# 128-wide attention: ScalarE in place of VectorE multiplies the exponentials by the reciprocal sums

## The chip, the cores and the metric

The kernel runs on one core of a Trainium2 chip. The metric is the device time of one execution in microseconds (us). Engines are written as the profile writes them: PE is TensorE, DVE is VectorE, ACT is ScalarE, POOL is GpSimd, SP is SyncE.

## What is computed

A decoder of two layers works on x, 16 sequences of 64 tokens of width 256, that is 1024 tokens or 8 tiles of 128 rows. It runs a self attention, a cross attention and a mixture of experts, then a causal attention, the attention that the change touches, and a second mixture of experts. The attention in question, cut to its core (H = 16 query heads, 4 key heads, HD = 128, 128 keys for each sequence: 64 of the context and 64 of its own):

```
q = rope(rms_norm(h @ Wq.T))           # 16 heads of 128
k = rope(rms_norm([ctx, h] @ Wk.T))    # 4 heads of 128
v = [ctx, h] @ Wv.T
scores = q @ k.T / sqrt(128)
probs  = softmax(scores)               # over the 128 keys
x      = x + (probs @ v) @ Wo.T
```

## The kernel before

`attention128` goes over the 8 tiles of 128 rows (two sequences each). Each engine has one program, written out by hand, and the engines meet at semaphores. `skewed` builds them: `early` for tile 0, then seven times `mixed(n, u, n1, u1)`, then `late` for tile 7. `mixed` handles the scores, softmax, values and projection of tile n interwoven with the projections, rope and transposes of tile n1 = n + 1. So in a period of `mixed` each engine works through a fixed list, in order, and an instruction that waits holds back everything behind it on its engine.

The softmax of a tile runs in four groups k = 0..3 of four head blocks of 128 x 128:

- PE `scores(n, k)` writes the bank `xps`; DVE `maxes(n, k)` (L1088, L1090) writes the negated scaled maxima `xnb`; ACT `exps(n, k)` (L798) computes four exponentials of 128 x 128 from PSUM into `E` (`xE` in the profile) with the bias per partition, and each leaves its row sum in `sm` by a second small instruction (ACTIVATION_READ_ACCUMULATOR), then raises `exp_ok`.
- DVE `normalise(n, k)` waits for `exp_ok`, takes the reciprocal of four sums (L1095, `rc_ok`), and multiplies the whole group, 128 x 512, by it in place (L1097), then raises `e_ok`.
- PE `turn_probs(n, k)` (L913) waits for `e_ok`, and for `t_out`, and transposes the four blocks into one of two PSUM banks `xpt`. ACT `pt_copy(n, k)` (L765, `xPT<-xpt`) copies them out and raises `t_out`. PE `pv(n, k)` (L925) multiplies by V; ACT `o_copy` (L808) copies that out; PE `project` (L933) applies Wo.

The two banks `xpt` are shared by all transposes of a period in a fixed order: the two key groups, the groups 0, 1 and 2 of the probabilities, a query group, group 3 of the probabilities, two more query groups, the next hidden tile, the last query group. Each transpose number j waits until copy number j - 2 is out, so `turn_probs(n, 3)` waits for `pt_copy(n, 2)`, and the query transpose behind it, `turn_qk(n1, 1)` (L943), for the query copy `qk_out` before it; that one also waits for `scale(n1, 1)` on DVE (L1083).

On ACT the second half of a period runs in this order: `exps(n, 2)`, `o_copy(n, 1)`, `square(n1, 6)` (L788), `exps(n, 3)`, `pt_copy(n, 2)`, `qk_out` 0, `v_copy(n1, 7)`, `pt_copy(n, 3)`. On PE: `turn_probs(n, 1)`, `pv` 0, `scores` 2, `pv` 1, `scores` 3, `fill(n1, 6)` (L896, six matmuls), `turn_probs(n, 2)`, `turn_qk(n1, 0)`, `fill(n1, 7)`, `turn_probs(n, 3)`, `turn_qk(n1, 1)`, `pv` 2.

POOL adds the two halves of the rope (`add`, L733, 128 x 512 from SBUF to SBUF) and takes the roots (L738, L727) in order.

Of the kernel before, what the change touches and what calls it, by code (L numbers as in the profile page):

```python
# [14 lines left out]
ALU = mybir.AluOpType  # L15
ACT = mybir.ActivationFunctionType
# [19 lines left out]
class Store:  # L36
# [7 lines left out]
    def sb(self, name, shape, dt=F32):  # L44
        return self.stack.enter_context(self.nc.sbuf_tensor(name, shape, dt))
# [18 lines left out]
def bcast(ap, axis, n):  # L64

    shape = list(ap.shape)
    shape.insert(axis, n)
    return ap.unsqueeze(axis).to_broadcast(shape)
# [475 lines left out]
KEYS = 2 * S  # L544
# [10 lines left out]
class Split:  # L555
# [9 lines left out]
    def share(self, n):  # L565
        return bass.ds(n * (self.COLS // NT), self.COLS // NT)
# [99 lines left out]
def attention128(nc, C, w):  # L666
# [5 lines left out]
    with m.stack:  # L672
# [16 lines left out]
        E = sb("xE", [P, XH, KEYS])  # L689
# [3 lines left out]
        rc = sb("xrc", [P, XH])  # L693
# [16 lines left out]
        def turns(n, u):  # L710

            base = n * STEP_T + FIRST_T
            if type(n) is int and n == NT - 1:
                base -= 1
                return base, lambda k: (base + k) % 2
            return base, lambda k: (u + k) % 2
# [6 lines left out]
        @block.gpsimd  # L723
        def _(pool):
            def root(n, u):
                pool.wait_ge(var_ok, n + 1)
                pool.tensor_tensor(mv[:, u, 3:4], mv[:, u, 2:3], neghalf[:, 0:1], ALU.pow).then_inc(rstd_ok, 1)  # L727

            def add(n, k):

                pool.wait_ge(rope_ok, n * 6 + k + 1)
                blk = qr[:, 4 * k:4 * k + 4, :]
                pool.tensor_tensor(blk, blk, t2[:, k % 2, :, :], ALU.add).then_inc(add_ok, 1)  # L733

            def rms_root(n, part):
                pool.wait_ge(ms_ok, n * 2 + part + 1)
                c = RMS[part]
                pool.tensor_tensor(sr[:, c], sv[:, c], neghalf[:, 0:1].to_broadcast([P, c.stop - c.start]), ALU.pow).then_inc(sr_ok, 1)  # L738

            def step(n1, u1):  # L740

                for k in range(4):
                    add(n1, k)
                rms_root(n1, 0)
                add(n1, 4)
                if type(n1) is not int or 1 <= n1 < NT - 1:
                    root(n1 + 1, 1 - u1)
                add(n1, 5)
                rms_root(n1, 1)

            root(0, 0)
            root(1, 1)
            step(0, 0)
            step(1, 1)
            with pool.Fori(0, (NT - 4) // 2) as i:
                step(i * 2 + 2, 0)
                step(i * 2 + 3, 1)
            step(NT - 2, 0)
            step(NT - 1, 1)

        @block.scalar
        def _(act):
            def turned(j, dst, src):
                act.wait_ge(t_ok, j + 1)
                act.activation(dst, src, ACT.Copy).then_inc(t_out, 1)  # L765

            def own(t):

                return t.rearrange("p c (b k) -> p c b k", b=2)

            def h_out(n, u, j, bank):

                act.wait_ge(t_ok, j + 1)
                act.activation(hs[:, u, 0, :, :], p_t[bank][:, 0:DC, :], ACT.Copy, scale=H_UP)
                act.activation(kv[:, u, 0, :, :, S:KEYS], own(p_t[bank][:, 0:DC, :]), ACT.Copy, scale=H_UP).then_inc(high_ok, 1)
                act.activation(kv[:, u, 0, :, :, 0:S], own(ctxT[:, :, bass.ds(n * P, P)]), ACT.Copy, scale=H_UP).then_inc(chigh_ok, 1)

            def qk_out(j, i, bank):
                if i < 4:
                    dst = QT[:, :, 4 * i:4 * i + 4, :]  # L780
                    turned(j, dst.rearrange("p b h q -> p h b q"), p_t[bank][:, :, :].rearrange("p h (b q) -> p h b q", b=2))
                else:
                    turned(j, KT[:, 4 * (i - 4):4 * (i - 4) + 4, :], p_t[bank][:, :, :])

            def square(n, k):

                act.wait_ge(r_ok, n * 8 + k + 1)
                act.activation(sq[:, SQI[k] % 2, :, :], p_r[k % 2][:, :, :], ACT.Square).then_inc(sq_ok, 1)  # L788

            def v_copy(n, u, k):  # L790
                act.wait_ge(r_ok, n * 8 + k + 1)
                act.activation(V[:, u, (k - 5) // 2, :, :], p_r[k % 2][:, :, :], ACT.Copy, scale=1.0 / (H_UP * W_UP)).then_inc(v_out, 1)

            def exps(n, k):
                act.wait_ge(nb_ok, n * 4 + k + 1)
                for i in range(4):
                    c = 4 * k + i
                    ins = act.activation(E[:, c, :], p_s[k % 2][:, i, :], ACT.Exp, bias=nb[:, c:c + 1], scale=XSCALE,  # L798
                                         accum_out=sm[:, c:c + 1])
                ins.then_inc(exp_ok, 1)  # L800

            def pt_copy(n, k, j, bank):
                turned(j, PT[:, k % 2, :, :], p_t[bank][:, :, :])

            def o_copy(n, u, k):

                act.wait_ge(o_ok, n * 4 + k + 1)
                act.activation(OT[:, 8 * (k % 2):8 * (k % 2) + 8, k // 2, :],  # L808
                               p_o[(u + k) % 2][:, :].rearrange("p (h q) -> p h q", q=S), ACT.Copy).then_inc(o_out, 1)

            def early(n, u):
                h_out(0, 0, 0, 0)
                for k in (0, 1, 2, 3, 4):
                    square(0, k)
                    if k == 1:
                        h_out(1, 1, 1, 1)
                v_copy(0, 0, 5)
                square(0, 6)
                v_copy(0, 0, 7)
                act.wait_ge(t_out, 2)  # L820
                for i in range(4):
                    qk_out(2 + i, i, i % 2)

            def mixed(n, u, n1, u1):
                base, bank = turns(n, u)
                square(n1, 0)
                qk_out(base + T_K[0], 4, bank(T_K[0]))
                square(n1, 1)
                qk_out(base + T_K[1], 5, bank(T_K[1]))
                square(n1, 2)  # L830
                exps(n, 0)
                square(n1, 3)
                exps(n, 1)
                square(n1, 4)
                pt_copy(n, 0, base + T_P[0], bank(T_P[0]))
                v_copy(n1, u1, 5)
                pt_copy(n, 1, base + T_P[1], bank(T_P[1]))
                o_copy(n, u, 0)
                exps(n, 2)
                o_copy(n, u, 1)  # L840
                square(n1, 6)
                exps(n, 3)
                pt_copy(n, 2, base + T_P[2], bank(T_P[2]))
                qk_out(base + T_Q[0], 0, bank(T_Q[0]))
                v_copy(n1, u1, 7)
                pt_copy(n, 3, base + T_P[3], bank(T_P[3]))
                qk_out(base + T_Q[1], 1, bank(T_Q[1]))
                o_copy(n, u, 2)
                qk_out(base + T_Q[2], 2, bank(T_Q[2]))
                if there(n + 2):  # L850
                    h_out(n + 2, u, base + T_H, bank(T_H))
                o_copy(n, u, 3)
                if there(n + 2):
                    act.wait_ge(t_out, base + T_H + 1)
                qk_out(base + t_q(n, 3), 3, bank(t_q(n, 3)))

            def late(n, u):
                base, bank = turns(n, u)
                qk_out(base, 4, bank(0))
                qk_out(base + 1, 5, bank(1))  # L860
                exps(n, 0)
                exps(n, 1)
                pt_copy(n, 0, base + 2, bank(2))
                pt_copy(n, 1, base + 3, bank(3))
                o_copy(n, u, 0)
                exps(n, 2)
                o_copy(n, u, 1)
                exps(n, 3)
                pt_copy(n, 2, base + 4, bank(4))
                pt_copy(n, 3, base + 5, bank(5))  # L870
                o_copy(n, u, 2)
                o_copy(n, u, 3)

            skewed(act, early, mixed, late)
# [154 lines left out]
        def _(dve):  # L1029
# [62 lines left out]
            def normalise(n, k):  # L1092
                c = slice(4 * k, 4 * k + 4)
                dve.wait_ge(exp_ok, n * 4 + k + 1)
                dve.reciprocal(rc[:, c], sm[:, c]).then_inc(rc_ok, 1)  # L1095
                dve.wait_ge(rc_ok, n * 4 + k + 1)
                dve.tensor_tensor(E[:, c, :], E[:, c, :], bcast(rc[:, c], 2, KEYS), ALU.mult).then_inc(e_ok, 1)  # L1097

            def residual(n, u):
                dve.wait_ge(proj_ok, n + 1)  # L1100
# [1168 lines left out]
```

## Time and profile before

| | us |
|---|---|
| median of 3 runs | 1067.71 (1065.79 to 1068.55) |
| the profiled execution | 1067.61 |
| its span, first to last instruction | 1065.8 |
| PE busy | 827.1 |
| DVE busy | 720.8 |
| ACT busy | 486.7 |
| POOL busy | 383.0 |

All durations below are from the one profiled execution; 1.8 us of its time lie outside its span. The attention that is touched runs from about 472 us to 763 us of the span. A row of the timeline gives start and length; a row with x4 is four instructions in a row, and the pitch of an engine is the distance from one start to the next, which is shorter than a length because consecutive instructions overlap.

### The profile page before, as it was taken

The page shows a single profiled execution, that of the slowest core. Times are in us where ns is not written, and L with a number is a line of the kernel's source. Part 1 is how long each engine was busy: PE and PEld are TensorE (multiplying, and loading weights), DVE is VectorE, ACT ScalarE, POOL GpSimd, SP SyncE. Part 2 cuts the span into 40 slices and gives each one's busy share as a digit, 9 for nine tenths or more (in the row PEclk, how much of TensorE's full clock was granted, in tenths as well). Part 3 has the DMA queues.
Part 4 walks back from the last instruction along what each step waited for, and adds up shares of the span by engine and source line. Part 5 has one row for each costly group of instructions (what it writes and reads, how often), then busy time and mean ns, then how long its engine had stood idle before and what let it go on. Part 6 is the DMA issues. An engine that isn't in the chain of part 4 may idle for free. (4 is left out here: it accounts for less than half of the span.)

```text
span 1065.8 us, 17161 instructions
## 1 busy us (share of the span) xinstructions
PE 827.1 (78%) x5527; PEld 542.3 (51%) x5534; DVE 720.8 (68%) x1503; ACT 486.7 (46%) x1241; POOL 383.0 (36%) x345
## 2 busy tenths in 40 slices
PE   3899752347777248957799888997549999999997
PEld 2777642216666136733567666676434444444443
DVE  3778956557999359837887788874355656656555
ACT  1765432114555225623654556555244554445453
POOL 1113763673555455505444344531021122121210
PEclk9999975568999669968999999999759999999999
DMA  9900001226988212000000000000106344343431
GB/s 312 419 15 2 2 2 60 80 76 207 283 264 273 84 45 58 22 1 1 1 1 1 1 0 0 1 1 1 48 11 172 109 123 119 109 133 103 133 94 40
DMA packets 49344, 90.63 MB, mean 85 GB/s; under 512 B 7046, under 2 KB 30089, under 8 KB 48778
## 3 DMA queue, kind: packets, MB, share of 16 engines
q1 hardware_dynamic: 46218, 81.63, 24.6%
q0 software_dynamic: 3072, 8.30, 2.5%
q8 instruction: 31, 0.51, 0.2%
q14 instruction: 23, 0.19, 0.1%
HBM read 67.71 MB, written 22.29 MB: 84 GB/s over the span
## 5 line engine op out<-in xcount | busy, mean ns | idle before, releaser
L1199 POOL TENSOR_TENSOR m1ws<-m1raw,m1ws 128x768 f16<-128x768 f32 x33 | 55.0, 1669 | 219.2 <-ACT m1raw L1202 219.2
L733 POOL TENSOR_TENSOR xqr<-xqr,xt 128x512 f32<-128x512 f32 x48 | 61.3, 1277 | 140.1 <-DVE xt L1069 140.1
L1509 DVE TENSOR_TENSOR m1sg<-m1sg,m1Wb 128x512 f32<-128x512 f32 x66 | 61.5, 931 | 63.5 <-ACT m1sg L1427 52.8
L1469 PE MATMUL m1pg<-m1hs,m1ws 128*128 128x512 f16 x396 | 97.5, 383 | 3.8 <-PEq L58 3.8
L1480 PE MATMUL m1py<-m1ap,m1ws 128*128 128x512 f16 x396 | 96.3, 379 | 1.4 <-DVE m1ap L1521 1.4
L1469 PE MATMUL m1pu<-m1hs,m1ws 128*128 128x512 f16 x396 | 97.1, 382 | 0.0
L1431 ACT ACTIVATE m1ap<-m1ac 128x512 f16<-128x512 f32 x66 | 41.6, 630 | 116.8 <-DVE m1ac L1515 116.8
L1521 DVE TENSOR_TENSOR m1ap<-m1ac,m1ap 128x512 f16<-128x512 f32 x66 | 45.7, 692 | 45.9 <-ACT m1ap L1431 45.9
L1469 PEld LDWEIGHTS m1pg<-m1hs,m1ws 128*128 128x128 f16 x396 | 38.9, 98 | 51.3 <-issue 5.3
L1480 PEld LDWEIGHTS m1py<-m1ap,m1ws 128*128 128x128 f16 x396 | 38.6, 98 | 48.7 <-DVE m1ap L1521 2.4
L1469 PEld LDWEIGHTS m1pu<-m1hs,m1ws 128*128 128x128 f16 x396 | 39.0, 99 | 47.7 <-issue 1.6
L788 ACT ACTIVATE xsq<-xpr 128x512 f32<-128x512 f32 x48 | 28.8, 601 | 75.3 <-PE xpr L896 75.3
L933 PE MATMUL xpo<-xwo,xOT 128*128 128x256 f32 x256 | 59.6, 380 | 0.7 <-ACT xOT L808 0.7
L1065 DVE TENSOR_REDUCE xss<-xsq 128x4 f32<-128x512 f32 x48 | 32.7, 682 | 35.1 <-ACT xsq L788 34.6
L798 ACT ACTIVATE xE<-xps,xnb 128x128 f32<-128x128 f32 x128 | 45.5, 380 | 23.5 <-DVE xnb L1090 23.5
L896 PE MATMUL xpr<-xparts,xhs 128*128 128x512 f16 x192 | 49.4, 397 | 8.1 <-DVE xkv L1049 5.2
L933 PEld LDWEIGHTS xpo<-xwo,xOT 128*128 128x128 f32 x256 | 47.1, 190 | 7.5 <-ACT xOT L808 1.3
L896 PE MATMUL xpr<-xparts,xkv 128*128 128x512 f16 x192 | 47.6, 387 | 3.4 <-DVE xt L1069 3.4
L2026 PE MATMUL m0ph<-m0xs,m0wg 128*128 128x256 f16 x384 | 48.7, 278 | 0.6 <-DVE m0xs L2074 0.6
L1612 POOL TENSOR_TENSOR m0wg<-m0rg,m0wg 128x512 f16<-128x512 f32 x32 | 37.0, 1156 | 33.9 <-DVE m0rg L2063 33.9
L2014 PE MATMUL m0px<-ident,m0xg 128*128 128x128 f32 x128 | 21.9, 299 | 34.1 <-DMA m0xg<-slots_in 34.0
L1427 ACT ACTIVATE m1sg<-m1pg 128x512 f32<-128x512 f32 x66 | 39.3, 596 | 17.5 <-PE m1pg L1469 17.5
(299 smaller groups left out, 2048.3 us busy)
## 6 DMA issues: line engine op xcount, KB each, us to landing
m1Wb<-wt_dram SPq DMA_DIRECT2D x66, 256.0 KB, 3.9
m1raw<-in_m_w SPq DMA_DIRECT2D x33, 384.0 KB, 4.3
slots_in<-zeros SPq DMA_DIRECT2D x1, 8192.0 KB, 26.4
m0rg<-in_m_wgu SPq DMA_DIRECT2D x32, 256.0 KB, 3.9
m0xg<-slots_in SPq DMA_DIRECT2D x32, 256.0 KB, 3.6
slots_out<-m0yo SPq DMA_DIRECT2D x32, 256.0 KB, 2.9
m0rd<-in_m_wd SPq DMA_DIRECT2D x32, 128.0 KB, 3.3
xwo<-in_x_wo SPq DMA_DIRECT2D x1, 2048.0 KB, 18.4
```

What stands on the lines that cost most here:

```text
L733: pool.tensor_tensor(blk, blk, t2[:, k % 2, :, :], ALU.add).then_inc(add_ok, 1)
L798: ins = act.activation(E[:, c, :], p_s[k % 2][:, i, :], ACT.Exp, bias=nb[:, c:c + 1], scale=XSCALE, accum_out=sm[:, c:c + 1])
L896: ins = pe.matmul(p_r[k % 2][:, :, :].rearrange("p h d -> p (h d)"), lhs, rhs, start=(i == 0), stop=(i == 5))
L933: ins = pe.matmul(p_o[u][:, 0:D], OT[:, h, :, :].rearrange("p b q -> p (b q)"), wo[:, h, :], start=(h == 0), stop=(h == XH - 1))
L1199: pool.tensor_tensor(ws[:, u, 1, :], raw[:, u, :], ws[:, u, 0, :], ALU.subtract).then_inc(prep_ok, 1)
L1427: act.activation(sg[:, q, :], p_g[q][:, :], ACT.Silu, scale=1.0 / (H_UP * W_UP)).then_inc(silu_ok, 1)
L1431: act.activation(ap[:, q, 0, :], ac[:, q, :], ACT.Copy).then_inc(ah_ok, 1)
L1469: ins = pe.matmul(bank[:, :], part(ws, u, sw, c, which), hs[:, sh, c, CH * q:CH * q + CH], start=(k == 0), stop=(k == 5))
L1480: ins = pe.matmul(p_y[c][q][:, :], ws[:, u, sw, GU + P * c:GU + P * c + P], ap[:, q, sa, :], start=(first and k == 0), stop=(last and k == ...
L1509: dve.tensor_tensor(sg[:, q, :], sg[:, q, :], Wb[:, u, CH * q:CH * q + CH], ALU.mult).then_inc(sw_ok, 1)
L1521: dve.tensor_tensor(ap[:, q, 1, :], ac[:, q, :], ap[:, q, 0, :], ALU.subtract).then_inc(al_ok, 1)
L2026: ins = pe.matmul(p_h[u][:, which, :], wg[:, u, sw, P * (2 * c + which):P * (2 * c + which) + P], xs[:, u, sx, c, :], start=(i == 0), stop ...
```

## The change

DVE keeps the reciprocal of the sums and loses the multiply L1097. ACT gets `share(n, k)`: it waits for the reciprocals (`rc_ok`) and runs four Copy activations of 128 x 128 in place on `E`, from SBUF to SBUF, each with one column of `rc` as its scale per partition, and raises `e_ok`. In `mixed`, `share` 0 stands behind `exps` 1, `share` 1 behind the next square, `share` 2 behind `square(n1, 6)` and ahead of `exps` 3, and `share` 3 right behind `exps` 3. In `late` shares 0 and 1 stand behind `exps` 1, and shares 2 and 3 behind `exps` 3.

```diff
+            def share(n, k):
+                act.wait_ge(rc_ok, n * 4 + k + 1)
+                for c in range(4 * k, 4 * k + 4):
+                    ins = act.activation(E[:, c, :], E[:, c, :], ACT.Copy, scale=rc[:, c:c + 1])
+                ins.then_inc(e_ok, 1)
...
                 exps(n, 1)
+                share(n, 0)
                 square(n1, 4)
+                share(n, 1)
                 pt_copy(n, 0, base + T_P[0], bank(T_P[0]))
...
                 exps(n, 2)
                 o_copy(n, u, 1)
                 square(n1, 6)
+                share(n, 2)
                 exps(n, 3)
+                share(n, 3)
                 pt_copy(n, 2, base + T_P[2], bank(T_P[2]))
...
                 exps(n, 0)
                 exps(n, 1)
+                share(n, 0)
+                share(n, 1)
...
                 exps(n, 3)
+                share(n, 2)
+                share(n, 3)
...
                 dve.reciprocal(rc[:, c], sm[:, c]).then_inc(rc_ok, 1)
-                dve.wait_ge(rc_ok, n * 4 + k + 1)
-                dve.tensor_tensor(E[:, c, :], E[:, c, :], bcast(rc[:, c], 2, KEYS), ALU.mult).then_inc(e_ok, 1)
```

## Rows read from the trace of the kernel before

**Rows 1.** groups of instructions, stage 505 to 755: names, shapes, count, busy, mean, idle before

```profile
L1097 DVE TENSOR_TENSOR xE<-xE,xrc 128x512 f32<-128x512 f32 x32 | 36.3, 1133 | 1.1
...
L913 PE MATMUL xpt<-ident,xE 128*128 128x128 f32 x128 | 20.7, 284 | 25.6 <-DVE xE L1097 25.6
```

**Rows 2.** PE in order of time, one tile: start us, us, what, [idle before, releaser]

```profile
613.43 0.60 PE L913 MATMUL xpt<-ident,xE 128*128 128x128 f32 x4
...
615.25 0.66 PE L913 MATMUL xpt<-ident,xE 128*128 128x128 f32 x4
...
621.76 0.66 PE L913 MATMUL xpt<-ident,xE 128*128 128x128 f32 x4 [1.04 <-DVE xE L1097]
...
625.75 0.65 PE L913 MATMUL xpt<-ident,xE 128*128 128x128 f32 x4 [1.60 <-DVE xE L1097]
626.35 0.66 PE L943 MATMUL xpt<-ident,xqr 128*128 128x128 f32 x4
...
658.83 0.65 PE L913 MATMUL xpt<-ident,xE 128*128 128x128 f32 x4 [1.60 <-DVE xE L1097]
```

**Rows 3.** DVE in order of time, the same tile

```profile
613.50 1.70 DVE L1097 TENSOR_TENSOR xE<-xE,xrc 128x512 f32<-128x512 f32 x1
...
618.83 0.40 DVE L1090 TENSOR_SCALAR xnb<-xmx 128x4 f32<-128x4 f32 x1
...
621.02 0.69 DVE L1097 TENSOR_TENSOR xE<-xE,xrc 128x512 f32<-128x512 f32 x1
...
623.92 1.70 DVE L1097 TENSOR_TENSOR xE<-xE,xrc 128x512 f32<-128x512 f32 x1
625.54 0.68 DVE L1083 TENSOR_TENSOR xqr<-xqr,xsr 128x512 f32<-128x512 f32 x1
```

**Rows 4.** POOL in order of time, the same tile

```profile
617.93 1.27 POOL L733 TENSOR_TENSOR xqr<-xqr,xt 128x512 f32<-128x512 f32 x1
...
623.80 1.26 POOL L733 TENSOR_TENSOR xqr<-xqr,xt 128x512 f32<-128x512 f32 x1 [3.57 <-DVE xt L1069]
```

**Rows 5.** ACT in order of time, the same tile

```profile
612.39 0.23 ACT L798 ACTIVATION_READ_ACCUMULATOR xE<-xps,xnb 128x1 f32 x1
...
619.26 0.37 ACT L798 ACTIVATE xE<-xps,xnb 128x128 f32<-128x128 f32 x1 [1.85 <-DVE xnb L1090]
...
620.56 0.22 ACT L798 ACTIVATION_READ_ACCUMULATOR xE<-xps,xnb 128x1 f32 x1
620.65 0.61 ACT L808 ACTIVATE xOT<-xpo 128x512 f32<-128x512 f32 x1
621.13 0.62 ACT L788 ACTIVATE xsq<-xpr 128x512 f32<-128x512 f32 x1
...
622.98 0.65 ACT L765 ACTIVATE xPT<-xpt 128x512 f32<-128x512 f32 x1
```

**Rows 6.** ACT in order of time, two stretches of the first layer

```profile
66.58 0.74 ACT L242 ACTIVATE a0qT<-a0pq,a_bq 128x128 f32<-128x128 f32 x2
67.08 0.52 ACT L261 ACTIVATE a0cT<-a0po 128x256 f32<-128x256 f32 x1
...
93.03 0.83 ACT L571 ACTIVATE xparts<-xraw 128x768 f16<-128x768 f32 x1
93.76 0.83 ACT L572 ACTIVATE xraw<-xraw 128x768 f32<-128x768 f32 x1
```

**Rows 7.** ACT, then PE, in order of time, last tile

```profile
741.46 0.24 ACT L798 ACTIVATION_READ_ACCUMULATOR xE<-xps,xnb 128x1 f32 x1
...
746.07 0.37 ACT L798 ACTIVATE xE<-xps,xnb 128x128 f32<-128x128 f32 x1 [1.22 <-DVE xnb L1090]
...
743.19 1.03 PE L925 MATMUL xpo<-xPT,xV 128*128 128x256 f32 x4
...
750.98 3.55 PE L925 MATMUL xpo<-xPT,xV 128*128 128x256 f32 x8
```

**Rows 8.** stretches of 1 us: length, PE busy, granted clock, DMA

```profile
751.00:752.00 1.00, 1.00 (x5) 0.50 0.00 0
```

## Prediction

> **What bounds the kernel now.** I read the groups of instructions of the touched stage first, because the change is confined to it. L1097 holds DVE for 36.3 us in 32 instructions, and PE stands idle for 25.6 us ahead of L913, the transposes that read what L1097 wrote [rows 1]. So the multiply is on PE's path, and DVE's total load is not what matters: the question is when `e_ok` rises in each group.
>
> The timelines of one tile answer that. A period of `mixed` lasts 658.83 - 625.75 = 33.08 us [rows 2], and PE is idle for 1.04 us ahead of the transposes of group 2 and 1.60 us ahead of those of group 3. Groups 0 and 1 (613.43, 615.25) hardly wait. On DVE [rows 3] the multiply takes 0.69 us for group 2 but 1.70 us for groups 1 and 3. The row of POOL tells why: its rope addition runs from 623.80 to 625.06 [rows 4], and L1097, issued at 623.92, ends at 625.62, 0.56 us after it. The two do not run side by side. The same addition holds L1090 (618.83, 0.40 us long) until POOL's previous one is over at 617.93 + 1.27 = 619.20 [rows 3, 4], and ACT's exponentials of group 2 start right behind that, at 619.26 [rows 5].
>
> So the path of a period's second half is: POOL's addition, L1090, exponentials 2 (619.26), one copy (620.65), one square (621.13), exponentials 3, L1095, L1097 of group 3 (ends 625.62), transposes 3 (625.75), transposes of the query (626.35). From 619.26 to 625.75 it is 6.49 us long [rows 2, 5].
>
> **The price of the new work.** A `share` is four ACTIVATEs of 128 x 128, SBUF to SBUF, with a pointer to the scale. No row shows that form, so I bound the pitch. From below: two ACTIVATEs of 128 x 128 from PSUM with a pointer as bias fill 66.58 to 67.08, 0.25 us each [rows 6]. What SBUF as source adds comes from the two of 128 x 768, SBUF, no pointer: pitch 0.73 [rows 6]. Against the copy of 128 x 512 from PSUM, pitch 0.48 [rows 5], and with lengths of 0.83 and 0.61 giving 0.22 us for 256 elements, 0.86 ns each, a 128-wide one would be 0.73 - 0.55 = 0.18 from SBUF and 0.48 - 0.33 = 0.15 from PSUM. So the pointer adds 0.10 and SBUF 0.03 to 0.04: the pitch is 0.28 to 0.29 us. I take 0.285, 1.14 us for a group, with its last one some 0.40 long. The lower end is 0.16 (a pointer for a scale costs nothing), the upper end 0.34 (that of an exponential with its accumulator row, four in 1.39 us, 619.26 to 620.65 [rows 5]).
>
> The Trainium skill, page "ScalarE: Activation LUTs", section "What ACT_TABLE_LOAD costs", says 186 ns plus 0.833 ns an element, about 93 more for each pointer operand, and 93 of overlap between neighbours, which makes 0.294 and would make the sum below some 0.6 us larger, by an estimate. Its section "Rules for kernel authors" wants multiplications on VectorE; the rows here agree only where POOL is quiet (0.69 against 1.14 us) and speak against it where POOL adds (1.70).
>
> **The steady period, step by step.** First half: exponentials 1 leave ACT free at 612.39 + 0.09 = 612.48. Share 0 ends at 612.48 + 3 x 0.285 + 0.40 = 613.74, so transposes 0 start at about 613.8 instead of 613.43. Share 1, behind the next square, ends near 615.4, and transposes 1 follow at 615.55 instead of 615.25. This puts PE 0.2 to 0.3 us later, all of it ahead of the wait at 621.76, which swallows it. DVE is freed, but L1090 of group 2 still waits for POOL, whose chain begins only 0.1 us earlier: exponentials 2 start at 619.15.
>
> Second half, on ACT: exponentials 2 1.39, copy 0.48, square 0.48 (PE's fill 6 is just done), share 2 1.14, exponentials 3 1.37. Then share 3 waits for L1095: the last accumulator row, the reciprocal and two handovers leave a gap of 0.38. Share 3 takes 1.14. Now the important line: `pt_copy` 2, which before went out at 622.98 [rows 5], is queued behind share 3 on ACT, and transposes 3 wait for its bank. It costs 0.61 and 0.05 to PE. The sum is 7.04, so transposes 3 start at 619.15 + 7.04 = 626.19 against 625.75. Behind them the query's transposes follow after 0.49 instead of 0.60, because L1083 (625.54 in [rows 3]) no longer comes last, though POOL's addition now delays it instead of L1097: 626.68 against 626.35. Each period loses 0.33 us. Transposes 2 are 1.1 us later than before (their multiply moved from DVE, in parallel, into ACT's queue behind a copy and a square), but they are hidden in front of transposes 3.
>
> There are seven `mixed`. In the first, DVE's queue was the limit in the first half and the relief there (0.7 us on the start of exponentials 2) cancels the loss: 0. The other six give 6 x 0.33 = 2.0 us.
>
> The last tile has nothing to hide behind. Exponentials 1 leave ACT at 741.46 + 0.09 = 741.55 [rows 7]; shares 0 and 1 take 2.28 and the copy 0.65, so `pv` 0 starts at 744.48 instead of 743.19, +1.29. Exponentials 2, 2.88 us behind `pv` 0 as before (746.07 - 743.19), start at 747.36. Then 1.39 + 0.48 + 1.37 + 2 x 1.14 + 0.65 = 6.17 bring `pv` 2 to 753.53 instead of 750.98: +2.55 us.
>
> The sum is 0 + 2.0 + 2.55 = +4.5 us. On the profiled execution's 1067.61 that is 1072.1; this execution is 0.1 under the median, so it stands for the median too. VectorE's relief of 36 us is otherwise worth nothing, since nothing else in the period ends last on it.
>
> **The rivals.**
> - *The shares are cheaper: pitch 0.25.* The pointer for a scale and the SBUF source then cost together what a pointer for the bias does. The same chain: the period loses 0.05 (0.3 in six), the first tile gains 0.4, the last loses 2.0: +1.9, 1069.5, no difference that can be measured. Not slower, and it speaks for it that it is the nearest row. About this point it turns: below 0.25 the periods gain.
> - *A scale pointer costs nothing: pitch 0.16.* Each period gains 0.67 (share 3's chain ends 625.19), six give 4.0, the first 0.6, the last loses 0.55: -4.1, 1063.5, faster. It needs what the pair with a bias pointer speaks against.
> - *The clock of PE falls once more.* In the last tile PE now waits 1.3 us longer ahead of `pv` 0 (1.29 above). Before, the granted clock fell to 0.50 (1.2 GHz) at 751, behind the thin stretch ahead of `pv` 2 [rows 8], and `pv` 2 and 3 took 3.55 us for 8 matmuls where 4 take 1.03 elsewhere [rows 7], some 1.7 us more. Once more of that for the block from `pv` 0 to `scores` 3 gives +6.2, 1073.8. Against it: the clock did not fall at that wait before. The fall at 751 may also end in the longer wait now, which would give 1 us back.
> - *The shares are as dear as exponentials: 0.34.* +8.5, 1076.1.
>
> **How the numbers follow.** Chances: the forecast 0.54 (1070.9 to 1073.3), pitch 0.25 0.22, free pointer 0.09, clock 0.12, dear shares 0.03. A run of this kernel can tell about 0.3% from no change, 3.2 us. Slower by more: 0.49 of the forecast's, 0.12, 0.01 and 0.03, that is 0.65. Within: 0.05 of the forecast's, 0.21 of the cheaper shares, 0.02 of the free pointer, that is 0.28. Faster: 0.07. The range runs from 1068.8, under the cheaper shares, to 1075.8, over the clock's case.
>
> **What would show it.** Right: a share's pitch of 0.28 to 0.29; a period of 33.4 us; transposes 2 about 1 us later in it, transposes 3 0.4 us later, released by ACT's copy of `xPT` and not by `e_ok`; the last tile 2.5 us longer. Wrong: a period under 33.1, transposes 3 released by ACT's `xE`, exponentials 2 starting more than 0.3 us earlier in the period (then VectorE's relief counts), or L1083 ending last.

## The result, and the profile after

| | before | after |
|---|---|---|
| median, 10 runs each on one chip | 1068.13 (1063.56 to 1070.71) | 1074.90 (1072.12 to 1077.56) |
| ratio to before, 95% interval | | 1.0065 (1.005 to 1.008) |
| span of the profiled execution | 1065.8 | 1074.4 |

The change costs 6.8 us, where +4.5 was forecast. The line of the profile with the engines' busy time (engine, us, share of the span, instructions) shows the exchange of load that was meant: DVE loses 34.7 us and ACT gains 34.5.

```profile
PE 830.5 (77%) x5534; PEld 545.4 (51%) x5534; DVE 686.1 (64%) x1471; ACT 521.2 (49%) x1369; POOL 376.6 (35%) x345
```

The groups of the touched stage (505 to 765 us; as in [rows 1]): ACT's new line L806 is 40.6 us long, and PE's idle time ahead of the transposes of the probabilities, L928 now, has grown from 25.6 to 32.4 us. 7.3 us of it are released not by the multiply but by ACT's copy of `xPT`.

```profile
L806 ACT ACTIVATE xE<-xE,xrc 128x128 f32<-128x128 f32 x128 | 40.6, 403 | 1.7 <-DVE xrc L1110 1.7
...
L928 PE MATMUL xpt<-ident,xE 128*128 128x128 f32 x128 | 22.8, 306 | 32.4 <-ACT xE L806 25.0 <-ACT xPT L765 7.3
```

PE in order of time, one tile of the steady period, answering to [rows 2]:

```profile
617.39 0.65 PE L928 MATMUL xpt<-ident,xE 128*128 128x128 f32 x4 [0.29 <-ACT xE L806]
...
619.17 0.60 PE L928 MATMUL xpt<-ident,xE 128*128 128x128 f32 x4
...
623.13 1.46 PE L911 MATMUL xpr<-xparts,xkv 128*128 128x512 f16 x6
626.43 0.66 PE L928 MATMUL xpt<-ident,xE 128*128 128x128 f32 x4 [1.85 <-ACT xE L806]
...
629.83 0.66 PE L928 MATMUL xpt<-ident,xE 128*128 128x128 f32 x4 [1.00 <-ACT xPT L765]
630.32 0.65 PE L958 MATMUL xpt<-ident,xqr 128*128 128x128 f32 x4
...
663.37 0.65 PE L928 MATMUL xpt<-ident,xE 128*128 128x128 f32 x4 [1.00 <-ACT xPT L765]
```

The period is 663.37 - 629.83 = 33.54 us (before 33.08). The wait ahead of transposes 2 has become 1.85 us (from 1.04), that ahead of transposes 3 1.00 us (from 1.60), and it now ends with `ACT xPT`, the copy for the bank. Transposes 0, which before did not wait, wait 0.29 us at 617.39, and fill 6 starts 15.32 us behind the tile's first scores (623.13 - 607.81) instead of 14.95 (619.26 - 604.31).

ACT in order of time, the same tile, answering to [rows 5]:

```profile
615.97 1.29 ACT L806 ACTIVATE xE<-xE,xrc 128x128 f32<-128x128 f32 x4
...
622.50 0.37 ACT L798 ACTIVATE xE<-xps,xnb 128x128 f32<-128x128 f32 x1 [1.22 <-DVE xnb L1105]
...
623.88 0.61 ACT L815 ACTIVATE xOT<-xpo 128x512 f32<-128x512 f32 x1
624.62 0.60 ACT L788 ACTIVATE xsq<-xpr 128x512 f32<-128x512 f32 x1
625.12 1.26 ACT L806 ACTIVATE xE<-xE,xrc 128x128 f32<-128x128 f32 x4
626.29 0.35 ACT L798 ACTIVATE xE<-xps,xnb 128x128 f32<-128x128 f32 x1
...
628.01 1.28 ACT L806 ACTIVATE xE<-xE,xrc 128x128 f32<-128x128 f32 x4 [0.24 <-DVE xrc L1110]
629.20 0.57 ACT L765 ACTIVATE xPT<-xpt 128x512 f32<-128x512 f32 x1
```

Four shares take 1.17 us from start to next start (625.12 to 626.29), 0.29 each. Between the copy (623.88) and the square (624.62) lie 0.74 us instead of 0.48: ACT waits for PE's fill 6, which ends at 623.13 + 1.46 = 624.59. The copy `xPT`, which before went out straight after exponentials 3, starts at 629.20 behind share 3.

DVE, then POOL, the same tile, answering to [rows 3, 4]:

```profile
621.57 0.69 DVE L1103 TENSOR_REDUCE xmx<-xps 128x4 f32<-128x512 f32 x1 [1.07 <-PE xps L920]
622.30 0.17 DVE L1105 TENSOR_SCALAR xnb<-xmx 128x4 f32<-128x4 f32 x1
...
627.80 0.18 DVE L1110 RECIPROCAL xrc<-xsm 128x4 f32<-128x4 f32 x1 [0.53 <-ACT xE L798]
627.90 1.20 DVE L1098 TENSOR_TENSOR xqr<-xqr,xsr 128x512 f32<-128x512 f32 x1
...
617.99 2.91 POOL L738 TENSOR_TENSOR xsr<-xsv,neghalf 128x16 f32<-128x16 f32 x1
620.87 1.27 POOL L733 TENSOR_TENSOR xqr<-xqr,xt 128x512 f32<-128x512 f32 x1
```

L1105, the maxima's scaling of group 2, takes 0.17 us instead of 0.40: POOL no longer holds it, since POOL's root took 2.91 us here (3.35 before) and the addition behind it was over at 622.14. L1098, the old L1083, is now the one that POOL's addition holds (1.20 instead of 0.68).

The last tile, ACT, then PE, answering to [rows 7]:

```profile
747.02 2.46 ACT L806 ACTIVATE xE<-xE,xrc 128x128 f32<-128x128 f32 x8
...
748.37 2.27 PE L928 MATMUL xpt<-ident,xE 128*128 128x128 f32 x8 [4.18 <-ACT xE L806]
750.44 1.61 PE L940 MATMUL xpo<-xPT,xV 128*128 128x256 f32 x4
...
758.50 2.27 PE L928 MATMUL xpt<-ident,xE 128*128 128x128 f32 x8 [3.81 <-ACT xE L806]
760.57 2.53 PE L940 MATMUL xpo<-xPT,xV 128*128 128x256 f32 x8
```

And stretches of 1 us of it (length, PE busy, granted clock, DMA), answering to [rows 8]:

```profile
747.00:748.00 1.00, 0.00 (x0) 1.00 0.00 0
...
749.00:750.00 1.00, 0.96 (x5) 0.50 0.00 0
...
760.00:761.00 1.00, 1.00 (x6) 0.50 0.00 0
```

PE stands idle for 4.18 us ahead of transposes 0 and for 3.81 us ahead of transposes 2, and both times its granted clock falls from 1.00 to 0.50 (2.4 to 1.2 GHz), so that the transposes, eight in 2.27 us, and `pv` 0, 1.61 instead of 1.03 us, run at half speed.

To compare profiles of different executions, whose spans ahead of the stage differ by up to 9 us, the stage is measured below from the start of its first scores to the start of the last residual addition on DVE: before 762.43 - 505.04 = 257.39 us, after 771.00 - 505.82 = 265.18, +7.79. It splits at the first scores of tiles 1 and 7, by the starts of PE's scores: first tile 33.11 before and 34.90 after (+1.79), six steady periods 198.62 and 201.53 (+2.91), last tile 25.66 and 28.75 (+3.09).

### The profile page after: what moved, and what is told of

The parts are those of the page before. It is cut to its first block and busy times, and to the rows that moved or that the text cites. A ratio compares the mean times of both kernels' runs of the same rounds, so it can differ in the third digit from the quotient of the medians.

```text
span 1074.4 us, 17264 instructions
## 1 busy us (share of the span) xinstructions
PE 830.5 (77%) x5534; PEld 545.4 (51%) x5534; DVE 686.1 (64%) x1471; ACT 521.2 (49%) x1369; POOL 376.6 (35%) x345
```

## The experiments

Each was run beside the kernel before on the same chip. Times of different groups of runs stem from different chips (the kernel before took 1073.02, 1064.86 and 1067.73 us in the three), so the ratio and the lengths within the stage are what is to be compared. Periods and stages are those of one profiled execution of each kernel.

| kernel | ratio to before (95%) | steady period | stage |
|---|---|---|---|
| before | 1 | 33.08 | 257.39 |
| after | 1.0065 (1.005 to 1.008) | 33.54 | 265.18 |
| after, again | 1.0083 (1.0062 to 1.0104) | 33.55 | 265.19 |
| copy ahead of share 3 | 1.0046 (1.0025 to 1.0066) | 33.22 | 262.19 |
| shares 0 and 1 only | 1.0052 (1.0028 to 1.0076) | 33.06 | 260.90 |
| shares 2 and 3 only | 1.0068 (1.0045 to 1.0091) | 33.56 to 33.94 | 264.94 |
| constant scale | 0.9963 (0.9941 to 0.9985) | 32.45 | 255.08 |
| after, PE kept busy | 1.0055 (1.0036 to 1.0074) | 33.55 | 261.72 |
| before, PE kept busy | 0.9993 (0.9982 to 1.0004) | 33.08 | 255.75 |
| share 2 ahead of the square | 1.0105 (1.0086 to 1.0123) | 33.83 | 271.59 |
| only group 3 on ACT | 0.9977 (0.9962 to 0.9993) | 32.49 | 254.28 |
| only group 3, PE kept busy | 0.9952 (0.9934 to 0.9971) | 32.48 | 251.92 |

The theory going in: in the steady period the loss is ACT's queue (shares, and the copy behind share 3); the rest is PE's clock, which falls at the longer waits of the first and the last tile. The rival: PE waits for the shares as such, and the copy and the clock don't matter.

**Copy ahead of share 3** (label `e1_copy_ahead`).

```diff
                 exps(n, 3)
-                share(n, 3)
                 pt_copy(n, 2, base + T_P[2], bank(T_P[2]))
+                share(n, 3)
```

> The changed kernel with one exchange in mixed: on ACT pt_copy 2 stands ahead of share 3 instead of behind it. Theory A (in the steady period transposes 3 wait for the bank that pt_copy 2 frees, and that copy is queued behind share 3): the copy fits into the gap of about 0.4 us in which ACT waits for the reciprocal, transposes 3 are released by ACT's xE and start 0.36 us earlier, the period falls from 33.54 to about 33.2 us, the time by 2.5 us to about 1072.4. Rival B (e_ok itself, the length of the shares, is what PE waits for in group 3): the period stays at 33.5.

ACT, then PE, one tile:

```profile
628.14 0.61 ACT L765 ACTIVATE xPT<-xpt 128x512 f32<-128x512 f32 x1
628.62 1.28 ACT L806 ACTIVATE xE<-xE,xrc 128x128 f32<-128x128 f32 x4
...
630.03 0.65 PE L928 MATMUL xpt<-ident,xE 128*128 128x128 f32 x4 [0.72 <-ACT xE L806]
```

The period fell to 33.22 us, and PE's releaser of transposes 3 is `ACT xE`. The copy fills the time in which ACT would wait for the reciprocal. So 0.32 of the 0.46 us a period were the copy's place in the queue, and an order on ACT that the change wrote, not the price of the multiply. The ratio, 1.0046, is compatible with that and too wide to prove it; the period proves it. The stage is 2.99 us shorter than after, but only 2.01 of that are the six periods. In the first tile PE's clock did not fall here: 32.87 us, where after took 34.90 and after with PE kept busy, below, 33.23. In the last, which the edit leaves as it was, the clock stayed low longer (29.80 us instead of 28.75).

**Shares 0 and 1 only, shares 2 and 3 only** (`e2_groups01`, `e3_groups23`): `share` returns at once for the other two groups, and DVE's `normalise` multiplies them as in the kernel before. The diff is that of the first; the second has (0, 1) in both places.

```diff
             def share(n, k):
+                if k in (2, 3):
+                    return
...
                 dve.reciprocal(rc[:, c], sm[:, c]).then_inc(rc_ok, 1)
+                if k in (2, 3):
+                    dve.wait_ge(rc_ok, n * 4 + k + 1)
+                    dve.tensor_tensor(E[:, c, :], E[:, c, :], bcast(rc[:, c], 2, KEYS), ALU.mult).then_inc(e_ok, 1)
```

> Only groups 0 and 1 are multiplied on ACT; groups 2 and 3 stay on DVE as in the kernel before. Theory A (shares 0 and 1 delay PE's fill 6 by about 0.35 us and with it square 6, but exponentials 2 start 0.26 us earlier, so that square 6 comes out even): a period of 33.1 us, as before; what is lost is lost in the first tile (PE's clock, up to 1.8 us) and ahead of pv 0 of the last (1.3 to 1.8 us): 1070 to 1071.5. Rival B (the first half's delay adds to the period): 33.4 us.

> Only groups 2 and 3 are multiplied on ACT; groups 0 and 1 stay on DVE. Theory A (the loss of the period comes from shares 2 and 3 in ACT's queue): a chain of 7.1 us from exponentials 2 to transposes 3 instead of 6.49, a period of 33.6 us, no fall of the clock in the first tile, the last tile 1.3 to 2.5 us longer: 1073 to 1074.5. Rival B (shares 0 and 1 bring the loss): a period of 33.1 us and 1070.

With shares 0 and 1 alone the period is 33.06 us (one of the six is 33.96, in which PE's granted clock fell behind a wait of 1.75 us), with shares 2 and 3 alone 33.56 where PE's clock does not fall: the loss of the period belongs to groups 2 and 3. Groups 0 and 1 on ACT delay PE's fills, but POOL's root is then as short as after, and POOL's addition no longer holds DVE's scaling of the maxima (0.17 us). With shares 2 and 3 alone the root takes 3.35 us and that scaling 0.39. The root with shares 0 and 1 alone:

```profile
620.54 2.91 POOL L738 TENSOR_TENSOR xsr<-xsv,neghalf 128x16 f32<-128x16 f32 x1
```

The period of 33.06 us says that the two cancel. In the kernel with shares 2 and 3 alone PE's clock falls in four of the seven `mixed` tiles, and the periods that hold such a fall are 33.9 us long; it shows in the row of fill 7 (L912, 2.28 us for six instead of 1.46), behind a wait of 2.23 us. Three tiles with the same wait have no fall:

```profile
627.53 1.12 PE L929 MATMUL xpt<-ident,xE 128*128 128x128 f32 x4 [2.23 <-ACT xE L807]
628.44 1.06 PE L959 MATMUL xpt<-ident,xqr 128*128 128x128 f32 x4
629.29 2.28 PE L912 MATMUL xpr<-xparts,xkv 128*128 128x512 f16 x6
```

**Constant scale** (`e4_no_pointer`): the shares multiply by a constant, so the probabilities are not divided by their sums; every wait stands.

```diff
-                    ins = act.activation(E[:, c, :], E[:, c, :], ACT.Copy, scale=rc[:, c:c + 1])
+                    ins = act.activation(E[:, c, :], E[:, c, :], ACT.Copy, scale=0.01)
```

> The changed kernel with a constant scale of 0.01 in the shares instead of a pointer to the reciprocals (the softmax is not normalised; everything else, all waits too, is kept). It prices the pointer. Theory A (pitch 0.29 with a pointer, about 0.20 without; eight shares lie on the period's path): a period of 32.5 us, below that of the kernel before, and 1065 to 1067. Rival B (the pointer costs nothing, SBUF to SBUF is what is dear): pitch stays at 0.29 and the period at 33.5.

ACT, then PE, one tile:

```profile
626.25 0.91 ACT L806 ACTIVATE xE<-xE 128x128 f32<-128x128 f32 x4 [0.24 <-DVE xrc L1110]
...
627.69 0.66 PE L928 MATMUL xpt<-ident,xE 128*128 128x128 f32 x4 [0.64 <-ACT xPT L765]
```

Four take 0.91 us instead of 1.28 from the first start to the last end, 0.20 us each in pitch, so a pointer adds 0.09 us an instruction. Eight of these lie on the period's path, and the period is 1.09 us shorter, below that of the kernel before: 0.80 between exponentials 2 and transposes 3 (627.69 - 621.16 = 6.53 instead of 7.33, eight pointers and 0.07 less of the wait for fill 6), and the 0.29 us that PE waited ahead of transposes 0, which is gone. This is close to the forecast's rival of a free pointer (there with a pitch of 0.16): 0.37% faster than before. So the price of the pointer decides the sign of the change. The last tile is longer than before even so, 28.03 us against 25.66. PE waits 3.31 us in it ahead of transposes 2, and yet the eight transposes behind that wait took 1.45 us where they take 2.27 after: here the granted clock stayed at 1.00.

```profile
753.61 1.45 PE L928 MATMUL xpt<-ident,xE 128*128 128x128 f32 x8 [3.31 <-ACT xE L806]
```

**PE kept busy in the waits** (`e5_busy`, with the changed kernel once more, `after_again`).

```diff
+            def keep_busy(count, dst):
+                for i in range(count):
+                    pe.matmul(dst, hs[:, 0, 0, 0, :], wq[:, 0, 0, 0:512], start=True, stop=True)
...
+                if type(n) is int and n == 0:
+                    keep_busy(10, p_o[1][:, :])
                 turn_probs(n, 0, base + T_P[0], bank(T_P[0]))
...
+                keep_busy(17, p_r[0][:, :, :].rearrange("p h d -> p (h d)"))
                 turn_probs(n, 0, base + 2, bank(2))
...
+                keep_busy(15, p_r[0][:, :, :].rearrange("p h d -> p (h d)"))
                 turn_probs(n, 2, base + 4, bank(4))
```

> The changed kernel with matmuls whose result nobody reads on PE where it waits longest: 10 ahead of transposes 0 of the first tile, 17 ahead of transposes 0 and 15 ahead of transposes 2 of the last (2.2, 3.7 and 3.2 us at 2.4 GHz, against waits of 2.5, 4.2 and 3.8 us). Theory A (beside the queue on ACT the change costs falls of PE's granted clock to 1.2 GHz at these waits: 1.6 us in the first tile, 0.5 and some 1.5 us in the last): the granted clock stays at 1.00 there, periods stay at 33.5, and the stage from the first scores to the last residual takes 261.5 to 262.5 us instead of 265.2, 2 to 3.5 us less time than the changed kernel in the same call. Rival B (the clock falls all the same, or what follows the waits is not bound by PE): no difference.

> The changed kernel once more, beside the two others on the same chip, for the comparison with the kernel with matmuls in its waits. Expected: a ratio of 1.005 to 1.008 to the kernel before, periods of 33.54 us; if the clock falls by chance, the first tile is 1.6 us shorter in one execution than in the other.

PE, last tile:

```profile
743.47 1.12 PE L940 MATMUL xpo<-xPT,xV 128*128 128x256 f32 x4
...
751.06 0.65 PE L928 MATMUL xpt<-ident,xE 128*128 128x128 f32 x4 [0.58 <-ACT xE L806]
...
752.70 1.99 PE L940 MATMUL xpo<-xPT,xV 128*128 128x256 f32 x8
```

The granted clock stayed at 1.00 through the whole stage, `pv` 2 and 3 take 1.99 us, and the stage is 261.72 us, 3.47 less than that of the changed kernel run beside it, with 3.85 us between the medians (1070.77 and 1074.62). Periods are unchanged. So the falls cost the changed kernel 3.5 us: its first tile is 33.23 us instead of 34.90, its last 26.90 instead of 28.75 (after: 28.75, after again: 28.70).

**Kernel before, PE kept busy** (`e7_before_busy`): 11 such matmuls ahead of transposes 0 of the last tile, 7 ahead of transposes 2, 4 ahead of transposes 3.

```diff
+                keep_busy(11)
                 turn_probs(n, 0, base + 2, bank(2))
...
+                keep_busy(7)
                 turn_probs(n, 2, base + 4, bank(4))
+                keep_busy(4)
                 turn_probs(n, 3, base + 5, bank(5))
```

> The kernel before with matmuls whose result nobody reads on PE in the last tile: 11 ahead of transposes 0, 7 ahead of transposes 2, 4 ahead of transposes 3. Theory A (the kernel before pays for a fall of the clock to 1.2 GHz in its last tile too: pv 2 and 3 took 3.55 us where they take 1.99 at 2.4 GHz): the last tile from its scores to the residual takes 24.0 us instead of 25.66, 1.6 us less time. With it, the changed kernel kept busy is 4 to 5 us slower than the kernel before, and 5.5 to 6 slower than this one. Rival B (filling one wait moves the fall to another place): no difference.

PE, last tile:

```profile
750.26 1.98 PE L925 MATMUL xpo<-xPT,xV 128*128 128x256 f32 x8
```

The last tile fell to 24.04 us as expected, so the kernel before paid 1.6 us there. The medians differ by only 0.07%, with an interval that holds both nothing and the expected 0.15%; whether the fall occurs in every execution is open. With both kernels kept busy the stage is 261.72 against 255.75 us: 5.97 us are the price of the change without the clock (one profiled execution of each, on different chips): first tile +0.11, periods +3.00, last tile +2.86.

**Share 2 ahead of the square** (`e9_share_first`).

```diff
-                square(n1, 6)
                 share(n, 2)
+                square(n1, 6)
                 exps(n, 3)
```

> The changed kernel with share 2 ahead of square 6 on ACT instead of behind it. ACT no longer waits for PE's fill 6 (0.26 us a period), and transposes 2 are released 0.75 us earlier. Theory A (DVE then ends last: its rope 5 starts 0.9 us later behind the square, and the reciprocal of group 3 stands behind that rope): share 3 starts 0.3 us later, a period of 33.8 to 33.9 us, 2 us slower than the changed kernel. Rival B (the 0.26 us on ACT are all that counts): a period of 33.3 us, 2 us faster.

DVE, then ACT, one tile:

```profile
628.81 0.17 DVE L1110 RECIPROCAL xrc<-xsm 128x4 f32<-128x4 f32 x1
...
629.01 1.28 ACT L806 ACTIVATE xE<-xE,xrc 128x128 f32<-128x128 f32 x4 [0.78 <-DVE xrc L1110]
```

ACT waits 0.78 us for the reciprocal of group 3, which stands behind DVE's rope 5, which waits for the square: 33.83 us a period. The exchange saves the wait for fill 6 and loses more on DVE. ACT's queue, PE's fills and DVE's rope stand so close here that a gain on one is a loss on the next. Measured from transposes 3 to transposes 3, two of its periods were 35.4 and 35.3 us long. In both PE's granted clock fell to 0.50 at transposes 3, behind waits of 2.11 (first tile, 36.76 us long) and 2.12 us, and the `pv` behind them took 1.91 us instead of 1.03. The other waits there, four of 2.03 us and one of 2.12, had no fall behind them. So the stage of 271.59 us and, as far as the other executions fell alike, the ratio hold more than the queue: the periods without a fall are 0.3 us longer than after's.

**Only group 3 of the mixed tiles on ACT** (`e6_only3`, and `e8_only3_busy` with the matmuls of `e7_before_busy` in the last tile). The multiply of group 3, 1.70 us long on DVE beside POOL's addition, moves; the others (that of group 1 is as long, but PE does not wait for it) and the last tile stay on DVE, and the copy is ahead of share 3.

```diff
             def share(n, k):
+                if k in (0, 1, 2) or (type(n) is int and n == NT - 1):
+                    return
...
+                pt_copy(n, 2, base + T_P[2], bank(T_P[2]))
                 share(n, 3)
-                pt_copy(n, 2, base + T_P[2], bank(T_P[2]))
...
+                if k in (0, 1, 2) or (type(n) is int and n == NT - 1):
+                    dve.wait_ge(rc_ok, n * 4 + k + 1)
+                    dve.tensor_tensor(E[:, c, :], E[:, c, :], bcast(rc[:, c], 2, KEYS), ALU.mult).then_inc(e_ok, 1)
```

> A version meant to beat both: DVE keeps the multiply for groups 0, 1 and 2 and for the whole last tile; ACT multiplies only group 3 of the mixed tiles, the one whose multiply took 1.70 us because POOL's addition runs then, with pt_copy 2 ahead of it. Theory A: transposes 3 come 0.5 us earlier than in the kernel before, the query transposes behind them 0.6 us earlier (then L1083, held by POOL, comes last), a period of 32.4 to 32.5 us, no more falls of the clock than before, 0.4% faster than the kernel before (1063 to 1064.5 where that takes 1067.7). Rival B (the wait of ACT for the reciprocal and the share together are as long as 1.70 us on DVE): a period of 33.0, no difference.

> The version with only group 3 of the mixed tiles on ACT, with the same matmuls in the waits of the last tile. Theory A: periods of 32.45 to 32.5 us as before, the last tile 24.0 us instead of the 26.4 of that version's profiled execution, so 0.3 to 0.5% faster than the kernel before. Rival B (the small gain of that version came from chance in the clock): no more than 0.2%.

ACT, PE, DVE and POOL, one tile of `e6_only3`:

```profile
618.04 0.65 ACT L765 ACTIVATE xPT<-xpt 128x512 f32<-128x512 f32 x1
618.98 1.28 ACT L807 ACTIVATE xE<-xE,xrc 128x128 f32<-128x128 f32 x4 [0.29 <-DVE xrc L1111]
...
620.38 0.65 PE L929 MATMUL xpt<-ident,xE 128*128 128x128 f32 x4 [1.17 <-ACT xE L807]
620.88 0.60 PE L959 MATMUL xpt<-ident,xqr 128*128 128x128 f32 x4
...
618.86 0.66 DVE L1099 TENSOR_TENSOR xqr<-xqr,xsr 128x512 f32<-128x512 f32 x1
...
618.87 1.78 POOL L733 TENSOR_TENSOR xqr<-xqr,xt 128x512 f32<-128x512 f32 x1 [3.56 <-DVE xt L1085]
```

The period is 32.49 us, 0.59 less than before, as expected. The kernel is 0.23% faster than before (0.4% was expected) and with its last tile kept busy 0.48%: in the profiled execution of the plain one the clock fell in the last tile, which took 26.43 us against 24.04 with PE kept busy, a loss of 2.4 us where the kernel before lost 1.6. Both beat both kernels.

## Why the prediction was right, and where it was off

The direction and the mechanism held: the change is slower by 0.65%, and transposes 3 wait for the copy queued behind share 3. The size was too small. The 1074.9 us lie in the range of 1068.8 to 1075.8, but above the forecast's own band of 1070.9 to 1073.3; the range reaches so far for the sake of one more fall of the clock in the last tile. That fall came, but the last tile paid hardly more to the clock than before (1.85 against 1.62 us); what carried the time above the band were longer periods and a fall in the first tile. To that extent the range held by luck. The steps:

- *Pitch of a share*, 0.285 from bounds of 0.28 and 0.29: measured 0.29 (1.17 / 4). Right. So was the split into 0.10 for the pointer (measured 0.09).
- *First half of the period*: "PE 0.2 to 0.3 us later, all of it ahead of the wait at 621.76, which swallows it". Only half right, and the step that failed. PE was 0.37 us later at fill 6. The wait ahead of transposes 2 swallows it on PE, but square 6 on ACT waits for fill 6, and that is on the path: 0.26 us.
- *Exponentials 2* were to start 0.11 us earlier in the period, and start 0.26 us earlier (14.69 us behind the first scores instead of 14.95). POOL's root got 0.44 us shorter, so that POOL is no longer last: DVE's maxima (L1103, 621.57) wait 1.07 us for PE's scores 2 and the exponentials follow them. This cancels part of the above.
- *Second half*: the chain from exponentials 2 to transposes 3 was to be 7.04 us and is 629.83 - 622.50 = 7.33; the difference is the 0.26 us of fill 6 and 0.03 from the shares. With the query's transposes 0.12 us closer behind (0.11 forecast) the period loses 7.33 - 6.49 - 0.26 - 0.12 = 0.46 us instead of 0.33, the six 2.9 instead of 2.0.
- *L1083 held by POOL instead of L1097*: right (1.20 us), and not on the path.
- *First tile*: 0 forecast, +0.11 with PE kept busy, but +1.79 in the profile: the clock, which the forecast looked for only in the last tile.
- *Last tile*: +2.55 forecast, +2.86 with both kept busy: `pv` 0 comes 1.38 us later (1.29 forecast), exponentials 2 another 0.10 behind it (0), and from there to `pv` 2 it is 1.37 us more (1.26). In the profiles it is +3.09, since the kernel before lost 1.6 us to the clock there and the changed one 1.85.
- *The rival of the clock* was taken as an alternative with 0.12 where it was an addition to the forecast. Its place in the first tile was missed: share 0 lengthens PE's wait there to 2.52 us. Together with the queue's 5.97 it gives the profile's 7.79: 5.97 + 1.67 + 1.85 of the changed kernel, less the 1.64 of the kernel before, is 7.85.

The term of the sum that was mis-sized most is thus the first tile (0 against 1.79), then the six periods (2.0 against 2.9).

## What to carry to other kernels

When work moves from one engine to another, write out the new queue and ask for each instruction behind the moved work who waits for it; here a copy whose input stood ready 2.1 us earlier (transposes 2 were done at 627.09, the copy went out at 629.20) waited behind the new work and set the period. Move only the piece that gains: of the four multiplies of a tile two were dear on VectorE (groups 1 and 3, 1.70 us instead of 0.69, because GpSimd's addition ran), and for one of these, group 3, TensorE waited. Moving that one alone, with the copy ahead of it, was faster than moving none or all. A delay that one wait swallows has to be followed to every other reader of the same engine before it is written off.

## What the runs showed of the hardware

- A pointer as scale costs ScalarE 0.09 us an ACTIVATE of 128 x 128, SBUF to SBUF (pitch 0.29 against 0.20). The Trainium skill, page "ScalarE: Activation LUTs", section "What ACT_TABLE_LOAD costs", gives about 93 ns for a pointer operand, and the trace agrees. The estimate of the whole pitch from its figures, 0.294 us, was nearer to the measured 1.17 / 4 than the 0.285 worked out from rows.
- DVE and POOL hold each other both ways. In `e6_only3` DVE's multiply of the rope starts 0.01 us ahead of POOL's addition, takes 0.66 us, and the addition takes 1.78 instead of 1.27; in the kernel before the addition was first (by 0.12 us) and DVE's multiply of group 3 took 1.70 instead of 0.69. The page "SBUF — State Buffer" of the Trainium skill, section "Who interferes with whom", tells of an exclusive lock for the one that issues first, and these rows agree.
- POOL's root of 128 x 16 took 2.91 us instead of 3.35 in the `mixed` tiles of every kernel in which DVE does not multiply groups 0 and 1 (after, twice, and with the copy ahead of share 3, shares 0 and 1 only, the constant scale, PE kept busy and share 2 ahead of the square: 2.89 to 2.93), and 3.35 or 3.36 in the five in which it does. No kernel parts the two groups, and why the root changes is open.
- PE's granted clock fell to 1.2 GHz behind every wait of 3.8 to 4.2 us of the last tile that was left empty, but not behind one of 3.31 us (constant scale, transposes 2 of the last tile, clock 1.00 from 749 to 758 us). Behind shorter waits it fell in some places only: after 2.52 us in the first tile of the changed kernel, and not in that tile with the copy ahead of share 3 (32.87 us long); after 2.56 us in the last tile with only group 3 on ACT, and not after 2.58 us at the same place in the kernel before, where it fell at 751 us [rows 8]; after 2.23 us in four of seven tiles with shares 2 and 3 only; after 2.11 and 2.12 us in two tiles with share 2 ahead of the square, and not after 2.12 us in a third; after 1.75 us in one of four tiles with shares 0 and 1 only. So no length of the wait alone parts the two cases here. A fall cost from some 0.35 us (a period of 33.9 instead of 33.56, shares 2 and 3 only) to 2.4 us (the last tile with only group 3 on ACT, 26.43 instead of 24.04), and the two in the last tile with the copy ahead of share 3 together 2.9 (29.80 instead of 26.90). Matmuls that nobody reads, put in the wait, kept the clock at 2.4 GHz.
